# Transposing the count matrix of a two-layer graph network by DMA instead of by matmul

## The reference

```
h = relu(layernorm(x))                              # 1250 x 1024
h = sigmoid(h @ wenc.T + benc)                      # 1250 x 500
agg[d] = sum over edges (s -> d) of weight * (h @ conv_weight)[s]
x = x + (agg + h @ lin_weight.T) @ wdec.T + bdec    # 1250 x 1024

h = relu(layernorm(x))
h = h @ W.T + b
row, col = (src, dst), with one loop (i, i) added for each node
deg[i] = number of entries with row == i
x = x + sum over entries of deg[row]^-0.5 * deg[col]^-0.5 * h[col], added up at row
```

## Time and profile before

| | |
|---|---|
| median of 3 runs | 492.23 us (490.9 to 492.59) |
| profiled execution | 490.67 us |
| its span, first to last instruction | 488.3 us, so 2.4 us lie around it |
| granted TensorE clock | 1.000 of full speed |
| busy: PE, PEld, DVE, ACT, POOL | 470.5, 407.7, 317.8, 199.5, 35.5 us |
| aggregation of layer 1, blocks 0 and 1 | 151.5 to about 224 us |
| DMA traffic | 66.33 MB, 136 GB/s on average |

### The profile page before, as it was taken

One profiled execution on the slowest core, in us unless ns is written; L12 is line 12 of the kernel. 1 busy time (PEld: TensorE's weight loads), 2 busy tenths in 40 slices (PEclk: granted clock), 3 DMA queues, 4 the chain that ended last, 5 costly groups with the idle time before them and its releaser, 6 DMA issues.

```text
span 488.3 us, 9494 instructions
## 1 busy us (share of the span) xinstructions
PE 470.5 (96%) x3636; PEld 407.7 (83%) x3636; DVE 317.8 (65%) x618; ACT 199.5 (41%) x397; POOL 35.5 (7%) x35
## 2 busy tenths in 40 slices
PE   1889999999999999999999999999999999999997
PEld 1889999988888778789978887888889988888885
DVE  7888897686865983542647878565634456567652
ACT  2847766655543212212524444355534522222220
POOL 4100000000000000000000000066510000000000
PEclk9999999999999999999999999999999999999999
DMA  8620114183110050043380002542787506545552
GB/s 309 236 77 11 56 65 148 55 324 120 64 65 13 1 210 1 1 161 135 156 292 0 1 1 70 190 173 87 302 303 323 196 1 238 215 173 200 181 189 90
DMA packets 22879, 66.33 MB, mean 136 GB/s; under 512 B 2384, under 2 KB 10842, under 8 KB 21170
## 3 DMA queue, kind: packets, MB, share of 16 engines
q1 hardware_dynamic: 22514, 65.30, 36.6%
q0 software_dynamic: 320, 0.39, 0.3%
HBM read 43.67 MB, written 22.01 MB: 135 GB/s over the span
## 4 chain that ended last, share of the span: by engine, by line
PE 86%; DVE 7%; ACT 4%; issue 1%; DMA 0%; POOL 0%; ACTq 0%; DVEq 0%; POOLq 0%
PE bank L1256 21%; PE bank L1257 20%; PE bank L1258 20%; PE bank L1272 18%; PE bank L1365 2%; DVE stats L921 1%; PE bank L1385 1%; PE bank L1480 1%; PE bank L1367 1%; PE bank L1369 1%; ACT h L752 1%; ACT we L765 1%; DVE h0T L1021 1%; DVE o_key L1014 1%; DVE before L941 1%
## 5 line engine op out<-in xcount | busy, mean ns | idle before, releaser
L1272 PE MATMUL bank<-a,h_hi 128*128 128x256 f16 (+3 forms) x400 | 85.6, 270 | 0.0
L1272 PE MATMUL bank<-a,h_lo 128*128 128x256 f16 (+3 forms) x400 | 85.6, 269 | 0.0
L1256 PE MATMUL bank<-right,left 128*128 128x512 f32 x140 | 54.6, 390 | 0.0
L1258 PE MATMUL bank<-right,left 128*128 128x512 f32 x140 | 54.5, 389 | 0.0
L1257 PE MATMUL bank<-right,left 128*128 128x512 f32 x140 | 54.5, 389 | 0.0
L1242 DVE SCALAR_TENSOR_TENSOR x<-bank,dis_u,x 128x512 f32<-128x512 f32 (+1 forms) x35 | 26.3, 752 | 38.4 <-PE bank L1258 38.4
L1256 PE MATMUL bank<-h0T,we 128*128 128x256 f32 (+3 forms) x160 | 47.2, 295 | 2.9 <-DVE hT L1028 1.5
L885 ACT CAST left<-zs 128x512 fp32r<-128x512 f32 x35 | 21.8, 625 | 64.3 <-PE bank L1258 64.3
L1257 PE MATMUL bank<-h0T,we 128*128 128x256 f32 (+3 forms) x160 | 45.8, 286 | 0.0
L1258 PE MATMUL bank<-h0T,we 128*128 128x256 f32 (+3 forms) x160 | 45.6, 285 | 0.0
L1256 PE MATMUL bank<-unit,g 128*128 128x500 f32 (+3 forms) x120 | 43.7, 364 | 0.8 <-DVE unit L1127 0.8
(11 more groups left out here) (152 smaller groups left out, 1100.9 us busy)
## 6 DMA issues: line engine op xcount, KB each, us to landing
right_scratch<-right SPq DMA_DIRECT2D x5, 2048.0 KB, 6.4
right<-right_scratch SPq DMA_DIRECT2D x5, 2048.0 KB, 8.4
whole<-w SPq DMA_DIRECT2D x7, 1024.0 KB, 9.1
adj_scratch<-stage SPq DMA_DIRECT2D x50, 125.0 KB, 1.8
raw<-adj_scratch SPq DMA_DIRECT2D x2, 2500.0 KB, 9.6
h<-x SPq DMA_DIRECT2D x9, 512.0 KB, 5.4
x<-x SPq DMA_DIRECT2D x9, 512.0 KB, 5.2
out<-x SPq DMA_DIRECT2D x18, 256.0 KB
```

Source lines behind the costliest of these rows:

```text
L1256: pe.matmul(o, lhs[0], rhs[0], start=first, stop=False, skip_group_check=True)
L1258: return pe.matmul(o, lhs[1], rhs[0], start=False, stop=last, skip_group_check=True)
L1272: ins = pe.matmul(o, h1[i][0:n, k, 128 * f:128 * (f + 1)], moving, start=(k == 0 and part == 0 and i == 0), stop=(k == T - 1 and part == p ...
```

## The change

Each tile's degree is followed on VectorE by the addition of the identity to the tile's diagonal block in `cnt` (after the sum has been read). Then SP issues one DMA per source tile with `transpose=True`, which writes the tile's 128 x 1280 counts turned over into `a2`. `cnt` and `a2` are widened from 1250 to 1280 columns, and GpSimd clears the 30 new columns of `cnt`. The DMAs of tiles 0 to 7 stand behind their degrees in block 0, ahead of the load of raw block 1; those of tiles 8 and 9 stand behind `("degrees",)` in block 1, followed by the load of `wd`, which now waits for all ten. The 110 matmuls, the 30 copies and their waits go. The second set of loads of the general path moves from SP to GpSimd, and GpSimd tests the flag once in each of the five column blocks of `z`.

```diff
-QS = ((0, 4), (4, 8), (8, 10))
+NODESP = P * T
@@ schedule()
-    turned = [("c", t, q) for t in range(T) for q in range(len(QS))]
         for k in range(T):
             steps += units[k + AHEAD:k + AHEAD + 1]
-            if turned and (n == 0 and k > 1 or n == 1):
-                steps += [turned.pop(0) for _ in range(2) if turned]
-                if not turned:
-                    steps += [("load", "wd")]
             steps += [("sk", n, k)]
             if n == 0:
-                steps += [("degree", k)]
+                steps += [("degree", k)] + ([("flip", k)] if k < T - 2 else [])
             if (n, k) == (1, 0):
-                steps += [("degrees",)]
+                steps += [("degrees",), ("flip", T - 2), ("flip", T - 1), ("load", "wd")]
@@ memory
-        cnt = at("cnt", [P, T, NODES], F16, R_C)
+        cnt = at("cnt", [P, T, NODESP], F16, R_C)
-        a2 = at("a2", [P, T, NODES], F16, R_OX)
+        a2 = at("a2", [P, T, NODESP], F16, R_OX)
@@ SP
+                elif s[0] == "flip":
+                    k = s[1]
+                    if k == 0:
+                        sp.wait_ge(stage_ready, NW)
+                        acc_done(sp, ("g", T - 1))
+                        sp.wait_ge(blank, 1)
+                    sp.wait_ge(loops_in, k + 1)
+                    sp.dma_start(a2[:, :, P * k:P * (k + 1)], cnt[:, k, :], transpose=True).then_inc(flipped, 16)
                 elif s == ("load", "wd"):
                     sp.wait_ge(deg_sums, 1)
-                    acc_done(sp, ("c", T - 1, len(QS) - 1))
+                    sp.wait_ge(flipped, 16 * T)
@@ GpSimd
+                    nc.gpsimd.memset(cnt[:, :, NODES:NODESP], 0.0).then_inc(blank, 1)
...
+                elif s[0] == "z" and s[2] == 0:
+                    b = s[1]
+                    m = pool.value_load(missed[0:1, 0:1], min_val=0, max_val=1)
+                    with pool.If(m != 0):
...
+                    pool.wait_ge(stage_ready, NW)
@@ VectorE
                 elif s[0] == "degree":
                     k = s[1]
                     dve.wait_ge(cnt_ready, NW)
-                    v.tensor_reduce(deg[:, k:k + 1], cnt[:, k, :], AX, ALU.add).then_inc(deg_parts, 1)
+                    v.tensor_reduce(deg[:, k:k + 1], cnt[:, k, 0:NODES], AX, ALU.add).then_inc(deg_parts, 1)
+                    n = tile_rows(k)
+                    dve.wait_ge(deg_parts, k + 1)
+                    v.tensor_tensor(cnt[:, k, P * k:P * k + n], cnt[:, k, P * k:P * k + n], ident16[:, 0:n], ALU.add).then_inc(loops_in, 1)
-                elif s[0] == "c":
...
-                    v.tensor_copy(a2[0:n, t, c0:c1], bank[banks_of[s]][0:n, 0:c1 - c0]).then_inc(bank_free, 1)
@@ TensorE: bias and every z wait for all ten DMAs
-                    read_done(pe, ("c", k, len(QS) - 1))
+                    pe.wait_ge(flipped, 16 * T)
-                elif s[0] == "c":
...
-                        ins = pe.matmul(oi, cnt[:, i, P * t:P * t + n], ident16[:, 0:w], start=(i == first), stop=(i != t),
-                                        skip_group_check=True)
-                        if i == t:
-                            ins = pe.matmul(oi, ident16[:, 0:n], ident16[:, 0:w], start=False, stop=True, skip_group_check=True)
```

More of the change, by code:

```diff
@@ L214, in schedule @@
         steps += [("s", n)]
-    assert not turned
     for t in range(T):
@@ L279, in build @@
             bank_for(("s", s[1], s[2]), *dense)
-        elif s[0] == "c":
-            bank_for(s, XBANKS, 8 - XBANKS)
         elif s[0] in ("t", "e", "g", "z", "bias", "edges"):
@@ L293, in build @@
                 bank_for((*s, i), *dense)
-        if s[0] in ("t", "e", "g", "c", "z", "bias", "s", "p", "o", "edges"):
+        if s[0] in ("t", "e", "g", "z", "bias", "s", "p", "o", "edges"):
             parts = {"s": KF, "p": 2}.get(s[0])
@@ L471, in build @@
         vec = sem("vec")
+        blank = sem("blank")
+        loops_in = sem("loops_in")
+        flipped = sem("flipped")
         starts_acc = sem("starts_acc")
@@ L512, in build @@
         rest_used = sem("rest_used")
+        rest_again = sem("rest_again")
         gen_rest = sem("gen_rest")
@@ L667, in _ @@
                             sp.wait_ge(rest_in, 16 * (b + 1))
[L668 to L673, removed]
                     sp.wait_ge(stage_ready, NW)
@@ L733, in _ @@
                     nc.gpsimd.memset(zs[:, :, NODES:ZCOLS], 0.0).then_inc(pad_ready, 1)
+                elif s[0] == "z" and s[2] == 0:
+                    b = s[1]
+                    m = pool.value_load(missed[0:1, 0:1], min_val=0, max_val=1)
+                    with pool.If(m != 0):
+                        acc_done(pool, ("z", b - 1, KD - 1) if b else ("bias",))
+                        nc.gpsimd.dma_start(a2_rest[:, :, 0:block_cols(b)], rest[:, :, B * b:B * b + block_cols(b)]).then_inc(rest_again, 16)
+                        pool.wait_ge(rest_again, 16 * (b + 1))
+                    pool.wait_ge(stage_ready, NW)
                 elif s[0] == "share":
@@ L1265, in layer1_z @@
                     pe.wait_ge(h1_ready, k + 1)
-                    read_done(pe, ("c", k, len(QS) - 1))
+                    pe.wait_ge(flipped, 16 * T)
                     for part in parts:
                         if part:
-                            pe.wait_ge(rest_in, 16 * (NB + b + 1))
+                            pe.wait_ge(rest_again, 16 * (b + 1))
                         moving = a2_rest[0:n, k, 0:c] if part else a2[0:n, k, B * b:B * b + c]
@@ L1470, in _ @@
                         ins.then_inc(unit_used, 1)
[L1471 to L1479, removed]
-                        ins = pe.matmul(oi, cnt[:, i, P * t:P * t + n], ident16[:, 0:w], start=(i == first), stop=(i != t),
-                                        skip_group_check=True)
-                        if i == t:
-                            ins = pe.matmul(oi, ident16[:, 0:n], ident16[:, 0:w], start=False, stop=True, skip_group_check=True)
-                    ins.then_inc(acc_ready, 1)
                 elif s[0] == "p":
```

## The result

The changed kernel takes 484.54 us (median of 4 runs, 482.82 to 484.76) against 492.27 us (490.9 to 492.59): ratio 0.9841, 95% interval 0.9811 to 0.987. The forecast was 485.4 us, faster, range 483.4 to 494. Its profiled execution took 484.76 us, its span is 483.0 us.

The account below looks back on a forecast made before the run. The prediction took PE (TensorE) as the bound: 490.67 us profiled, minus 6.8 us of PE's line, plus 0 for the rest, gave 483.9 us, or a 485.4 us median on the same footing; range 483.4 to 494 us.

Parts of the forecast that it names:

- a pair of `c` steps on PE: Two transposing-matmul steps between products of source tiles in blocks 0 and 1: each pair holds PE's line 0.455 us.
- PE's line, 15 pairs: Removing 8 pairs in block 0 and 7 in block 1 shortens PE's line by 6.8 us, between 5.6 and 7.4.
- addition of the loop on VectorE: Block 0, behind each degree: adding the 128 x 128 identity takes 0.3 us; cost to the kernel nothing, at most 0.6 us.
- clearing on GpSimd: Clearing 128 x 300 elements behind the gathers at the start fits within 0.87 us of idle time and costs nothing.
- T, one flip in a row: Time one tile's transposing DMA holds the SP queue ahead of raw block 1: 2.5 us, bounds 1.1 to 18.
- T from which raw block 1 is late: Up to 3.6 us of queue time per transposing DMA costs nothing; each further 0.1 us costs 0.8 us.
- raw block 1, issue to landing: The load queued on SP behind block 0's transposing DMAs lands 8.4 us after the queue is free.
- cover left on raw block 1: Landing at 182.4 us against a need by 188.5 us, ahead of product (1, 0): 6 us left.
- span to device time: Whole kernel: 2.4 us from span to device time; before the change, span 488.3 us and profiled execution 490.67 us.
- What bounds: In blocks 0 and 1 PE is busy throughout, so a removed matmul saves its place in PE's line: 6.8 us altogether.
- The queue: SP queue ahead of raw block 1: eight transposing DMAs leave it free at 174.0 us, needed by 180.1; nothing is late.
- The footing: Whole kernel: the median lies 1.56 us above the profiled execution, so 483.9 us profiled becomes a median of 485.4 us.

Follow-up runs that it names:

- three-fold: The changed kernel with every transposing DMA of block 0 issued three times, the extra ones into spare memory: 497.96 us, ratio 1.0129.
- two-fold: The changed kernel with every transposing DMA of block 0 issued twice, the second time into spare memory: 483.85 us.
- the second set of runs: The changed kernel again, unaltered, in the same session as later experiments: 483.28 us, ratio 0.9824.
- two experiments: The changed kernel with block 0's transposing DMAs issued three times, 497.96 us; and with each transposing DMA split into ten of 128 x 128, 561.28 us.
- the cuts of `wd`: The changed kernel with the four cuts of `wd` in block 1, behind products 4 to 7, instead of block 2: 481.52 us, ratio 0.9814.

## Why the prediction was right, step by step

| step | predicted | measured |
|---|---|---|
| a pair of `c` steps on PE | 0.455 us | 0.48 us |
| PE's line, 15 pairs | -6.8 us | -7.2 us |
| addition of the loop on VectorE | 0.3 us | 0.23 us |
| clearing on GpSimd | below 0.87 us, hidden | 0.36 us, hidden |
| T, one flip in a row | 2.5 us (1.1 to 18) | 1.62 us |
| T from which raw block 1 is late | 3.6 us | three-fold, 4.9 us per tile: late; two-fold, 3.2 us: not |
| raw block 1, issue to landing | 8.4 us | 10.2 us |
| cover left on raw block 1 | 6 us | 5.6 us |
| span to device time | +2.4 us | +1.8 us |
| median | 485.4 us | 484.54 us |

- **What bounds.** PE bound both blocks, and a matmul taken out shortened the kernel by its place in the line. The estimate was 6% low. In block 0 the first pair was worth 0.49 us and the other seven 0.46 each, and the product behind the last of them was 0.08 us slower (3.81 us in all, where 8 x 0.455 is 3.64). In block 1, which the prediction took from block 0, a pair was worth 3.39/7 = 0.48 us.
- **The queue.** The price of the flips was the open term, with a cover of 3.6 us against it. It was in the lower part of its bounds, and the changed kernel doesn't even meet it in block 0: flips 0 to 7 leave 21.02/8 = 2.63 us apart, since SP waits for their degrees (11.3 us in all), so T was not what spaced them. The value that I took (a small write's latency plus the rest of the bytes at the raw block's rate) came from two terms that don't describe what happens: in a row it goes with the engines busy at 205 GB/s, and singly it is SP's 1.3 us of issue. The rate is lower than the raw block's 300 GB/s (2500 KB in 8.4 us).
- **The figure from the Trainium skill** ("DMA: Bandwidth & Descriptors", "Latency and other measured facts"), 261 GB/s, stood nearer: the estimate from it was 1.3 us, where my own was 2.5. The trace has 205 GB/s and 1.62 us.
- **Landing of raw block 1.** 10.2 and not 8.4 us; without any flip it was 9.6, and in the kernel before 8.4. The cover absorbed it; the term was too small, and its cause stays open.
- **The footing.** I carried the 1.56 us between profiled execution and median of before over to after as scatter. More likely it was the clock's drop, which the profiled run of before had not and its median runs, by their times, had. The median after has it too (483.0 us of span at clock 0.996), so the transfer held. That was luck: in the second set of runs only one of five was in the upper group, and its median, 483.28 us, lies below the range that the prediction gave.
- **Outside the span.** The runs of the changed kernel and of the kernels made from it have 1.8 to 1.9 us around the span, those of before and of the kernel made from it 2.3 to 2.4. The half microsecond is outside what the trace shows; its cause stays open. With the 0.4 us of PE's line it makes up the 0.9 us between forecast and result.

## What to carry to other kernels

When work moves from a full engine to a queue, the gain is read on the engine and the risk on the queue: find the next transfer behind it that someone needs, work backwards to when the queue must be free, and divide by the number of new DMAs; that gives the price which they may have, and one run with twice and one with three times the DMAs shows how far the kernel is from it. Turn over as much as possible with one transposing DMA, since each cost SyncE about 1.3 us at 320 KB as at 32 KB. When memory comes free earlier, look what had been waiting for it: here the cuts of `wd` were worth another 1.4 us. And compare runs of equal clock, or the share of runs in each group moves the median by more than a small change is worth.

## What had not been expected of the hardware

- A transposing DMA of 320 KB and one of 32 KB hold SyncE for 1.34 and 1.29 us; they land after 3.4 and 2.4 us.
- Transposing DMAs in a row move some 205 GB/s within the core's memory with the DMA engines nine tenths busy or more, 1.62 us for 320 KB.
- In five of nine traces the granted clock falls from full to half right behind 100 matmuls of two columns (2.8 us in which PE counts as busy), for 3 to 4 us; what decides it is open. It also falls during the long waits of PE (11.38 and 75 us) that two experiments made, and stays at half for 3.4 and 6.0 us of work after their end, a loss of 1.7 and 3.0 us.
